# Behind the attention: x loaded early, norms' chains as bursts with a root step of third order, normed tiles turned and logits formed half a step later

## The chip, the core and the metric

The kernel runs on 1 core of one Trainium2 chip. It is one program with one launch. The metric is the device time of that core in microseconds (us); lower is better. A run of the kernel gives one time, and the median of several runs is what counts.

## What is computed

Two layers over 8 x 56 = 448 tokens of width 256 (S = 56), with a context of 1500 rows for each of the 8 batches. Cut to what matters here:

```python
x = x + attention0(layernorm(x), ctx)      # 16 heads of 128, softmax over 1500 keys, then @ Wo
x = x + moe0(layernorm(x))                 # 8 experts of 176 units, 2 chosen, plus 352 shared units
x = x + attention1(layernorm(x), ctx)      # linear attention, 16 heads of 16, 64 features, biases
x = x + moe1(layernorm(x))                 # 8 experts, 2 chosen, plus 704 shared units with a sigmoid gate

def moe(x):
    probs = softmax(x @ router)            # the two largest are kept; moe1 divides them by their sum
    h = silu(x @ w_gate) * (x @ w_up)      # all experts side by side: 1408 + shared columns
    return (h * weight_of_its_expert) @ w_down
```

layernorm subtracts the mean and multiplies by 1 / sqrt(variance + 1e-5).

## The kernel before

The program has three parts. The first forms sums over the context for the linear attention, and queries. The second is the softmax attention of layer 0, batch by batch, in a loop that all engines share. The third, from about 1034 us on, is what follows the attention: the output projection with Wo, three more norms, two mixtures of experts and the linear attention between them. All the edits lie in the third part and at the end of the second. Products there use a value split into a high and a low part and three matmuls (`mm3`, L104 to L106), so each weight and each activation has a high copy, made by ScalarE, and a low rest, made by VectorE or GpSimd.

**Tokens.** The 448 tokens are four tiles of 112 (`TP`), x is held as `[112, 4, 256]`, and the third part works on two halves (h = 0, 1) of two tiles each. A half's norm, router, linear attention and expert products follow each other; the halves are staggered, so that the small work of one half lies beside the expert products of the other.

**Output projection.** `wo.project(t, i)` forms tile t from quarter i of the heads, 12 matmuls each, t by t. `wo.add` (L1018) adds x to two finished tiles. The first norm (`ln1`) of half 0 is turned on TensorE between tiles 2 and 3. x is loaded by SyncE (L1783) behind the first layer's expert weights (L1290 to L1294: gate, up and down, 1.8 MB each, and 96 rows of down on their own) and behind a wait for the last output of the attention, since its tile takes the place of the attention's value weights.

**A norm** (class `Norm`): on VectorE `statistics` (L786, L789), `variance` (L803), a first value of the root (`guess`, L819, by the bits of the number; for the first half of the first norm ScalarE does it by Ln and Exp, L809 and L811), three Newton steps (`sharpen`: L828, L830, L833 each; one step after ScalarE's value), `apply` (L840, two tiles). Then `turn` on TensorE (L849), and from its PSUM bank `high` (L864) and `copy` (L869) on ScalarE and `low` (L876) on VectorE. Each small instruction waits for the one before it.

**A router** (class `Router`): `logits` (TensorE, L1140, from the norm's copy), `start` (VectorE, L1178 to L1183), `exponentials` (ScalarE, L1157 and L1159), `shares` (L1190 to L1194), `ranks` (L1203 to L1209), `weights` (L1216 to L1232), `turn` (TensorE, L1149), `high` (ScalarE, L1165), `low` (VectorE, L1171). ScalarE switches its table for Exp and again for Silu.

**Experts** (class `Experts`): the units are blocks of 128, 14 blocks in the first layer and 17 in the second. Step k is one block for one half; the steps go layer by layer, half by half: 28 and 34. For a step: `widen` (TensorE, 12 matmuls of gate and up), `silus` (ScalarE, L1411), `hidden` (VectorE, L1432), `spread` (TensorE, L1388, the token weights laid over the units), `weigh` (VectorE, L1444), `high` (ScalarE, L1423), `low` (VectorE, L1451), `narrow` (TensorE, 6 matmuls of down). `widen` of step k needs `hidden` of step k - 2. Weights of a block are split by `split_high` (ScalarE, L1340, L1343, L1346) and `split_low` (GpSimd, L1354, L1357, L1360).

**The order** is written out by hand: every engine runs a loop over positions n = 0 to 63 and does at each position the pieces that the functions `widen_at`, `spread_at`, `narrow_at` and `split_at` and the `if` lines give it. Step k is widened at position k, and as a rule spread there and narrowed three positions later. Position 28 (`FIRST1`) is where the second layer's steps begin, 45 (`SECOND1`) where those of its second half do. The second norm, the linear attention (`lin.query` L1539, `features`, `read`, `project`) and the third norm of half h sit at r = n - `BASE[h]`, with BASE = (15, 30). An engine runs its queue in order: whatever waits holds all that is behind it.

The last norm's first half is turned at position 28 ahead of everything else there, between the down projections of steps 26 and 27.

## Time and profile before

| | us |
|---|---|
| median of 3 runs (lowest to highest) | 1268.29 (1268.07 to 1269.38) |
| the profiled execution | 1267.16 |
| its span, first to last instruction | 1265.3 |
| TensorE busy | 1183.0 (93%) |
| VectorE busy | 880.1 (70%) |
| ScalarE busy | 740.6 (59%) |
| GpSimd busy | 536.7 (42%) |
| mean granted clock of TensorE | 0.982 of full speed |
| the part from 1034 us on | 231 |

The profile is one execution, recorded instruction by instruction. "Busy" is the time in which an engine has an instruction under way; a matmul's record reaches past the start of the next one, since they are pipelined. The granted clock is 1.0 at TensorE's higher level (2.4 GHz) and half of that at the lower (1.2 GHz). An engine that waits is shown with the instruction that released it. PEld is TensorE's weight load and runs beside the matmuls. SPq is SyncE's queue, which issues the transfers.

### The profile page before, as it was taken

Reading aid. Unit: us, or ns where it says so; the run is one execution under the profiler, and the core shown is the slowest. Engines: PE = TensorE matmul, PEld = TensorE weight load, DVE = VectorE, ACT = ScalarE, POOL = GpSimd, SP = SyncE. Lnnn points to the kernel's source line nnn. Section 1 sums busy time; section 2 is a strip of 40 time slices with the busy share of each in tenths; the row PEclk is TensorE's granted clock in tenths of the full one; section 3 lists DMA queues with packets and bytes.
Section 4 is the critical chain, followed back from the end, with each engine's and each line's share of the span. In section 5 each row is a group of like instructions: output and inputs, shape, how many; then the busy total and the mean of one; then the engine's idle time right before and its main releaser. Section 6 shows DMA issues by size and latency. Waiting matters only on the chain.

```text
span 1265.3 us, 28266 instructions
## 1 busy us (share of the span) xinstructions
PE 1183.0 (93%) x10014; PEld 1055.5 (83%) x10014; DVE 880.1 (70%) x1950; ACT 740.6 (59%) x1330; POOL 536.7 (42%) x561
## 2 busy tenths in 40 slices
PE   5999999999969999999999999999999996998988
PEld 4899999998848888888788788887888896887888
DVE  5766666666657888878878788788777643666564
ACT  3666666666545666576566665765666643544432
POOL 1533232323235363553643635535445764634400
PEclk9999999999989999999999999999999998999999
DMA  4211111100031111011010110111001024023000
GB/s 144 76 43 57 41 40 50 56 26 1 2 102 46 49 50 50 1 49 49 28 38 31 49 49 0 49 49 37 11 0 51 18 112 127 2 68 109 1 9 9
DMA packets 42689, 56.12 MB, mean 44 GB/s; under 512 B 3410, under 2 KB 41602, under 8 KB 42626
## 3 DMA queue, kind: packets, MB, share of 16 engines
q1 hardware_dynamic: 41810, 54.23, 13.6%
q10 hardware_dynamic: 816, 1.05, 0.3%
q8 instruction: 40, 0.66, 0.2%
q14 instruction: 23, 0.19, 0.0%
HBM read 54.81 MB, written 0.46 MB: 44 GB/s over the span
## 4 chain that ended last, share of the span: by engine, by line
PE 57%; DVE 7%; DMA 2%; issue 2%; ACT 2%; SPq 1%; POOL 1%; DVEq 0%; ACTq 0%
PE att_bank L104 16%; PE att_bank L106 15%; PE att_bank L105 15%; PE att_bank L1858 6%; PE att_bank L1816 3%; DMA att_raw_n<-in_ctx 1%; DVE att_cn L2113 1%; DVE att_pr L2167 1%; DMA tail_x<-in_x 1%; SPq L1294 1%; DVE tail_full L1432 1%; PE att_bank L1570 1%; DVE tail_hid L1451 0%; PE att_bank L943 0%; PE att_bank L1388 0%
## 5 line engine op out<-in xcount | busy, mean ns | idle before, releaser
L2339 POOL TENSOR_TENSOR att_sq<-att_work,att_sq 128x500 fp32r<-128x500 f32 x90 | 119.9, 1332 | 159.9 <-DVE att_sq L2133 159.9
L2343 POOL TENSOR_TENSOR attention_kk<-att_work,attention_kk 128x500 fp32r<-128x500 f32 x90 | 121.9, 1355 | 153.9 <-DVE attention_kk L2141 153.9
L104 PE MATMUL att_bank<-att_pT,att_cn 125*128 125x448 f32 x384 | 156.9, 409 | 5.5 <-DVE att_pT L2182 4.8
L1996 ACT ACTIVATE att_pr<-att_pr,att_nmx 112x1500 f32<-112x1500 f32 (+1 forms) x96 | 108.5, 1130 | 71.8 <-DVE att_nmx L2170 71.8
L106 PE MATMUL att_bank<-att_pT,att_cn 125*128 125x448 f32 x384 | 140.8, 367 | 0.0
L105 PE MATMUL att_bank<-att_pT,att_cn 125*128 125x448 f32 x384 | 140.4, 366 | 0.0
L2182 DVE TENSOR_TENSOR att_pT<-att_bank,att_pT 125x448 fp32r<-125x448 f32 x192 | 118.2, 616 | 14.6 <-ACT att_pT L2012 14.3
L2167 DVE TENSOR_SCALAR_CACHE_REDUCE att_pr<-att_bank 112x500 f32<-112x500 f32 x192 | 121.7, 675 | 6.3 <-PE att_bank L106 4.9
L1858 PEld LDWEIGHTS att_bank<-all_ident,att_pr 112*125 112x125 f32 x768 | 109.6, 189 | 14.2 <-ACT att_pr L1996 2.1
L538 DVE SCALAR_TENSOR_TENSOR attention_kk<-kvs_keys_ps,kvs_bk,attention_kk 64x500 fp32r<-64x500 f32 x96 | 70.9, 738 | 61.2 <-ACT attention_kk L422 59.3
L1858 PE MATMUL att_bank<-all_ident,att_pr 112*125 112x112 f32 x768 | 111.2, 271 | 1.7 <-ACT att_pr L1996 1.7
L293 PE MATMUL kvs_feat<-kvs_f,attention_kk 128*125 128x256 f32 x768 | 108.0, 283 | 4.5 <-ACT kvs_kp L475 4.3
L1985 ACT ACTIVATE att_work<-att_bank,att_eps 128x500 f32<-128x500 f32 x90 | 60.7, 675 | 86.7 <-PE att_bank L106 86.7
L2012 ACT ACTIVATE att_pT<-att_bank 125x448 fp32r<-125x448 f32 x192 | 102.2, 532 | 12.2 <-PE att_bank L1858 12.2
L681 POOL TENSOR_TENSOR attention_ct<-attention_raw_t,attention_ct 128x1000 fp32r<-128x1000 f32 x23 | 53.9, 2342 | 117.2 <-ACT attention_ct L414 117.2
L293 PEld LDWEIGHTS kvs_feat<-kvs_f,attention_kk 128*125 128x125 f32 x768 | 98.0, 187 | 6.2 <-ACT kvs_kp L475 4.0
L475 ACT ACTIVATE kvs_kp<-kvs_feat,kvs_zero 125x512 f32<-125x512 f32 x96 | 66.1, 689 | 59.7 <-PE kvs_feat L293 58.5
L2136 DVE TENSOR_TENSOR att_work<-att_bank,att_work 128x500 f32<-128x500 f32 x90 | 60.9, 676 | 56.4 <-ACT att_work L1992 55.7
L422 ACT ACTIVATE attention_kk<-kvs_keys_ps,kvs_bk 64x500 fp32r<-64x500 f32 x96 | 64.7, 674 | 52.6 <-PE kvs_keys_ps L106 51.2
L104 PE MATMUL att_bank<-attention_kk,attention_q 128*112 128x500 f32 x192 | 77.6, 404 | 17.1 <-DVE att_pr L2167 11.9
L1990 ACT ACTIVATE att_work<-att_bank,att_eps 128x500 f32<-128x500 f32 x90 | 61.1, 679 | 46.2 <-PE att_bank L1816 46.2
L104 PEld LDWEIGHTS att_bank<-att_pT,att_cn 125*128 125x128 f32 x384 | 73.2, 191 | 15.7 <-DVE att_pT L2182 9.9
(279 smaller groups left out, 3418.9 us busy)
## 6 DMA issues: line engine op xcount, KB each, us to landing
attention_raw_t<-in_ctxT SPq DMA_DIRECT2D x45, 500.0 KB, 3.9
att_raw_n<-in_ctx SPq DMA_DIRECT2D x16, 750.0 KB
kvs_raw_q<-in_wq SPq DMA_DIRECT2D x8, 256.0 KB, 3.9
tail_wo_raw<-in_wo SPq DMA_DIRECT2D x4, 512.0 KB, 4.4
tail_down_w<-in_down SPq DMA_DIRECT2D x8, 256.0 KB, 4.2
tail_gate_w<-in_gate SPq DMA_DIRECT2D x7, 256.0 KB, 2.8
tail_up_w<-in_up SPq DMA_DIRECT2D x7, 256.0 KB, 3.2
tail_gate_w<-in_gate SPq DMA_DIRECT2D x1, 1760.0 KB, 7.0
```

The lines of the kernel that those rows point to most:

```text
L104: nc.tensor.matmul(out, w_lo, x_hi, start=start, stop=False, skip_group_check=True)
L105: nc.tensor.matmul(out, w_hi, x_lo, start=False, stop=False, skip_group_check=True)
L106: return nc.tensor.matmul(out, w_hi, x_hi, start=False, stop=stop, skip_group_check=True)
L293: last = nc.tensor.matmul(feat[0:KP, half, z], ks[:, c, 2 * half + g, y], f2[:, w, :], start=(w == 1), stop=(w == 0), skip_group_check=True)
L538: nc.vector.scalar_tensor_tensor(ks[64:128, c, 2 * m + h, :], keys_ps[y, 0:CH], bk[y, m:m + 1], ks[0:64, c, 2 * m + h, :].bitcast(F32), AL ...
L1858: last = nc.tensor.transpose(ring[0:KP, t % 3, j * TP:(j + 1) * TP], pr[:, j, t * KP:(t + 1) * KP], ident[0:TP, 0:TP])
L1996: nc.scalar.activation(pr[:, j, keys], pr[:, j, keys], ACT.Exp, scale=-1.0, bias=nmx[:, j:j + 1], accum_out=z[:, 4 * u + j, c:c + 1]).then ...
L2012: nc.scalar.activation(pT[0][:, t % 3, :], ring[0:KP, t % 3, 0:QU], ACT.Copy).then_inc(pT_hi, 1)
L2167: nc.vector.tensor_scalar(pr[:, j, c * CH:(c + 1) * CH], ring[0:TP, c, 0:CH], -1.0, 3.0e38, ALU.mult, ALU.min, accum_out=mn[:, j, c:c + 1] ...
L2182: nc.vector.tensor_tensor(pT[1][:, t % 3, :], ring[0:KP, t % 3, 0:QU], pT[0][:, t % 3, :].bitcast(F32), ALU.subtract).then_inc(ring_free, 1)
L2339: nc.gpsimd.tensor_tensor(sq[1][:, i % 2, :], work[:, i % 2, :], sq[0][:, i % 2, :].bitcast(F32), ALU.subtract).then_inc(sq_lo, 1)
L2343: nc.gpsimd.tensor_tensor(kk[:, c, 2 + gi, :], work[:, i % 2, :], kk[:, c, gi, :].bitcast(F32), ALU.subtract).then_inc(k_lo, 1)
```

## The change

- x is loaded by SyncE as soon as two quarters of Wo are split (`wo_lo[1]`, `wo_lo[2]`), ahead of the expert weights. Its tile moves to the place of those quarters' raw weights.
- The first layer's expert weights are loaded as a head (5 blocks of gate, up and down) and a rest. A split of one of the first five blocks waits for all three head loads, a later one for all four of the rest.
- ScalarE does three weight splits, not two, ahead of the first root value, and the fifth one ahead of the first router's exponentials.
- `refine` takes the place of three `sharpen`: a step of third order in four instructions and one of second order in three, 7 in place of 9. For ln1's half 1, ln2 and ln3, statistics, root and normed tiles stand in one position and no longer in two (in ln1's half 1 the statistics stay two positions ahead).
- `ln2.turn` moves up within its position, ahead of the down projection, and `lin.query` to the end of the same position (half a position earlier). The rest of the linear attention comes one position earlier.
- `ln3`: its chain at r = 10, turned at r = 12 ahead of the down projection, logits at the end of r = 12. The router's start and exponentials are first in position r = 13, shares and ranks last in it; the weights come first in r = 14, the turn in the middle of r = 14. Half 0's turn, formerly at the head of position 28, is now handled as half 1's is.
- Down projections of steps 24 to 27 lie at positions 27, 28, 29 (behind the router's turn) and 29. The spreads of the second half's first steps are no longer held back to positions 48 to 50.
- Weight splits move a little: those of positions 14 to 16 to 12 to 14; 25, 28 and 31 are free, 26, 29, 30 and 32 to 38 are used.

```diff
-        return 4 if h == 0 and self.scalar_first else 11
+        return 4 if h == 0 and self.scalar_first else 9
...
+    def refine(self, dve, h):
+        nc, y, n = self.nc, self.half(h), self.first(h) + 2
+        rstd, tmp, var = self.rstd[:, y], self.tmp[:, y], self.var[:, y]
...
+        nc.vector.tensor_tensor(tmp, rstd, rstd, ALU.mult).then_inc(self.newton, 1)
+        nc.vector.tensor_tensor(tmp, tmp, var, ALU.mult).then_inc(self.newton, 1)
+        nc.vector.scalar_tensor_tensor(tmp, tmp, -10.0 / 3.0, tmp, ALU.add, ALU.mult).then_inc(self.newton, 1)
+        nc.vector.scalar_tensor_tensor(rstd, tmp, 5.0, rstd, ALU.add, ALU.mult).then_inc(self.newton, 1)
+        nc.vector.tensor_tensor(tmp, rstd, rstd, ALU.mult).then_inc(self.newton, 1)
+        nc.vector.scalar_tensor_tensor(tmp, tmp, -0.5 * 0.375 ** 3, var, ALU.mult, ALU.mult).then_inc(self.newton, 1)
+        nc.vector.scalar_tensor_tensor(rstd, tmp, 0.5625, rstd, ALU.add, ALU.mult).then_inc(self.newton, 1)
...
 def spread_at(k):
-    late = {0: 1, FIRST1: 29, SECOND1: 48, SECOND1 + 1: 48, SECOND1 + 2: 49, SECOND1 + 3: 49, SECOND1 + 4: 50}
-    return late.get(k, widen_at(k))
+    return {0: 1, FIRST1: FIRST1 + 1}.get(k, widen_at(k))
 def narrow_at(k):
-    return {FIRST1 // 2 - 1: k + 2, FIRST1 - 2: FIRST1, FIRST1 - 1: FIRST1, len(STEPS) - 1: k + 2}.get(
-        k, k + 3 if spread_at(k) == k else spread_at(k) + 2)
+    return {0: k + 3, FIRST1 // 2 - 1: k + 2, FIRST1 - 1: k + 2, len(STEPS) - 1: k + 2}.get(k, k + 3)
...
+        if m == 0 and n < HEAD:
+            act.wait_ge(self.head_loaded, 48)
+        elif m == 0:
+            act.wait_ge(self.rest_loaded, 64)
...
+        x = over_raw("x", [TP, TT, D])
...
+            sp.wait_ge(wo.wo_lo[1], 1)
+            sp.wait_ge(wo.wo_lo[2], 1)
+            sp.dma_start(x[:], a["x"].rearrange("(t p) d -> p t d", p=TP)).then_inc(x_loaded, 16)
             sp.wait_ge(pv_done, 2 * B * KT)
             sp.wait_ge(wo.wo_lo[3], 1)
-            moe.load_first(sp, a["gate0"], a["up0"], a["down0"])
-            sp.wait_ge(out_full, 2 * B)
-            sp.dma_start(x[:], a["x"].rearrange("(t p) d -> p t d", p=TP)).then_inc(x_loaded, 16)
+            moe.load_head(sp, a["gate0"], a["up0"], a["down0"])
+            moe.load_rest(sp, a["gate0"], a["up0"], a["down0"])
...
@@ TensorE's loop, in its new order
                 if n == FIRST1 + 1:
                     router.turn(pe, 2)
+                    moe.narrow(pe, FIRST1 - 2)
...
+                    if r == 3:
+                        ln2.turn(pe, h)
...
+                    if r == 12:
+                        ln3.turn(pe, h)
+                    if r == 14 and h == 1:
                         router.turn(pe, 3)
                 for k in steps_at(narrow_at, n):
...
                     if r == 3:
+                        lin.query(pe, h)
+                    if r == 12:
+                        router.logits(pe, 2 + h, ln3)
...
@@ ScalarE
+                for h in range(H):
+                    if n - BASE[h] == 13:
+                        router.exponentials(act, 2 + h)
+                if n == FIRST1 + 1:
+                    router.high(act, 2)
                 for k in steps_at(widen_at, n):
                     moe.silus(act, k)
...
@@ VectorE
+                for h in range(H):
+                    r = n - BASE[h]
+                    if r == 13:
+                        router.start(dve, 2 + h)
+                    if r == 14:
+                        router.weights(dve, 2 + h)
+                if n == FIRST1 + 1:
+                    router.low(dve, 2)
                 for k in steps_at(widen_at, n):
                     moe.hidden(dve, k)
...
                         ln2.statistics(dve, h, moe.added, h + 1)
                         ln2.guess(dve, h)
-                        ln2.sharpen(dve, h, 0)
+                        ln2.refine(dve, h)
                         ln2.apply(dve, h)
...
                     if r == 12:
+                        ln3.low(dve, h)
+                    if r == 13:
+                        router.shares(dve, 2 + h)
+                        router.ranks(dve, 2 + h)
```

## Rows read from the trace of the kernel before

**Rows 1.** Waits after 1034 us: total us, times, longest

```profile
PE att_bank L849 <- DVE tail_scratch L840: 16.8, 6, 8.7
```

**Rows 2.** Stages: us; PE, PEld, DVE, ACT, POOL busy; PEclk; DMA

```profile
1051.20:1069.10 17.90, 9.23 (x61) 9.23 (x62) 7.21 (x19) 6.83 (x19) 8.85 (x14) 0.71 0.24 60
...
1150.00:1168.00 18.00, 12.35 (x89) 11.31 (x88) 11.56 (x46) 9.91 (x24) 4.60 (x7) 0.91 0.42 131
...
1209.00:1229.00 20.00, 16.15 (x126) 15.23 (x126) 10.76 (x44) 7.91 (x16) 0.00 (x0) 0.91 0.00 1
```

**Rows 3.** Timeline of TensorE: start us, us, operation, [idle before <-releaser]

```profile
1045.27 0.28 PE L106 MATMUL att_bank<-tail_wo,tail_o_high 128*112 128x256 f32 x1
...
1050.89 0.28 PE L106 MATMUL att_bank<-tail_wo,tail_o_high 128*112 128x256 f32 x1
...
1059.87 1.01 PE L849 MATMUL att_bank<-all_ident,tail_scratch 112*128 112x112 f32 x4 [8.70 <-DVE tail_scratch L840]
...
1060.89 0.41 PE L105 MATMUL att_bank<-tail_wo,tail_o_high 128*112 128x256 f32 x1
...
1064.73 0.41 PE L105 MATMUL att_bank<-tail_wo,tail_o_high 128*112 128x256 f32 x1
```

**Rows 4.** Timeline of VectorE and ScalarE: the first norm's chain

```profile
1054.41 0.69 DVE L1018 TENSOR_TENSOR tail_x<-tail_x,att_bank 112x512 f32<-112x512 f32 x1 [10.50 <-DMA tail_x<-in_x]
...
1056.52 0.29 ACT L809 ACTIVATE tail_ln_rstd<-tail_ln_var,tail_zero 112x2 f32<-112x2 f32 x1 [2.40 <-DVE tail_ln_var L803]
...
1058.30 1.51 DVE L840 TENSOR_SCALAR tail_scratch<-tail_x,tail_ln_mv,tail_ln_rstd 112x256 f32<-112x256 f32 x2
```

**Rows 5.** GpSimd, SyncE, ScalarE; transfers (KB each, us to landing)

```profile
1028.81 4.75 POOL L980 TENSOR_TENSOR tail_wo<-tail_wo_raw,tail_wo 128x1024 fp32r<-128x1024 f32 x2
...
1033.65 0.37 SPq L1290 DMA_DIRECT2D tail_gate_w<-in_gate  x1
...
1041.83 0.95 ACT L986 ACTIVATE tail_o_high<-all_qT 128x896 fp32r<-128x896 f32 x1 [7.94 <-DVE all_qT L1001]
...
1052.78 0.42 ACT L1346 ACTIVATE tail_high_w<-tail_down_w 128x256 fp32r<-128x256 f32 x1 [5.88 <-DMA tail_down_w<-in_down]
...
tail_gate_w<-in_gate SPq DMA_DIRECT2D x1, 1760.0 KB, 7.0
...
tail_x<-in_x SPq DMA_DIRECT2D x1, 448.0 KB, 11.3
```

**Rows 6.** Timeline of TensorE at ln2's turns

```profile
1116.01 0.28 PE L1388 MATMUL att_bank<-tail_combT,tail_member 128*128 128x224 f32 x1
...
1119.15 0.60 PE L849 MATMUL att_bank<-all_ident,tail_scratch 112*128 112x112 f32 x4 [2.17 <-DVE tail_scratch L840]
...
1176.52 0.60 PE L849 MATMUL att_bank<-all_ident,tail_scratch 112*128 112x112 f32 x4 [3.12 <-DVE tail_scratch L840]
```

**Rows 7.** Timeline of VectorE in the norms' chains

```profile
1174.07 0.57 DVE L830 SCALAR_TENSOR_TENSOR tail_ln_tmp<-tail_ln_tmp,tail_ln_var 112x2 f32<-112x2 f32 x1
...
1207.19 0.74 DVE L786 BATCH_NORM_STATS2 tail_ln_stats<-tail_x 112x6 f32<-112x256 f32 x2
...
1208.59 0.16 DVE L828 TENSOR_TENSOR tail_ln_tmp<-tail_ln_rstd 112x2 f32<-112x2 f32 x1
```

**Rows 8.** Timeline around the second layer's routers

```profile
1156.34 0.18 DVE L1178 COPY tail_logit<-att_bank 112x18 f32<-112x18 f32 x1 [0.33 <-PE att_bank L1140]
...
1157.48 1.28 ACT L1411 ACT_TABLE_LOAD   x1
...
1158.78 0.45 ACT L1411 ACTIVATE tail_silu<-att_bank,tail_zero 128x224 f32<-128x224 f32 x1
...
1162.18 0.36 PE L1149 MATMUL att_bank<-all_ident,tail_comb 112*9 112x112 f32 x2 [3.11 <-DVE tail_comb L1232]
...
1223.67 0.28 DVE L1216 TENSOR_REDUCE tail_places<-tail_rank 112x16 f32<-112x128 f32 x1
...
1225.12 0.36 PE L1149 MATMUL att_bank<-all_ident,tail_comb 112*9 112x112 f32 x2 [1.30 <-DVE tail_comb L1232]
```

More of the change, by code:

```diff
@@ L1919, in _ @@
             for n in range(POSITIONS):
-                if n == FIRST1:
-                    moe.narrow(pe, FIRST1 - 3)
-                    moe.narrow(pe, FIRST1 - 2)
-                    ln3.turn(pe, 0)
-                    moe.narrow(pe, FIRST1 - 1)
-                    router.logits(pe, 2, ln3)
                 for k in steps_at(widen_at, n):
@@ L1965, in _ @@
                     if r == 3:
-                        ln2.turn(pe, h)
-                    if r == 13 and h == 1:
-                        ln3.turn(pe, 1)
-                        router.logits(pe, 3, ln3)
+                        lin.query(pe, h)
+                    if r == 12:
+                        router.logits(pe, 2 + h, ln3)
         @block.scalar
@@ L2047, in _ @@
             moe.split_high(act, 1)
+            moe.split_high(act, 2)
             ln1.guess_on_scalar(act, 0)
[L2049 removed]
+            moe.split_high(act, 3)
             ln1.high(act, 0)
             ln1.copy(act, 0)
[L2052 removed]
+            moe.split_high(act, 4)
             router.exponentials(act, 0)
[L2054 removed]
             for n in range(POSITIONS):
[L2056 to L2060 removed]
+                for h in range(H):
[3 more added lines that the diff above has]
+                    router.high(act, 2)
                 for k in steps_at(widen_at, n):
                     moe.silus(act, k)
[L2063 to L2064 removed]
                 if n == 1:
@@ L2072, in _ @@
                     router.high(act, 1)
-                if n == BASE[1] + 17:
-                    router.high(act, 3)
                 for i in split_at(n):
@@ L2085, in _ @@
                         ln2.copy(act, h)
+                        lin.query_on_scalar(act, h)
                     if r == 4:
-                        lin.query_on_scalar(act, h)
+                        lin.feature_on_scalar(act, h, 0)
                     if r == 5:
-                        lin.feature_on_scalar(act, h, 0)
-                    if r == 6:
                         lin.feature_on_scalar(act, h, 2)
-                    if r == 9:
+                    if r == 8:
                         lin.copy(act, h)
-                    if r == 13 and h == 1:
+                    if r == 12:
+                        ln3.copy(act, h)
                         ln3.high(act, h)
-                        ln3.copy(act, h)
                     if r == 14 and h == 1:
-                        router.exponentials(act, 3)
+                        router.high(act, 3)
         @block.vector
@@ L2243, in _ @@
             for n in range(POSITIONS):
-                if n == FIRST1:
-                    moe.low(dve, FIRST1 - 1)
-                    ln3.low(dve, 0)
-                    router.start(dve, 2)
-                    router.shares(dve, 2)
-                    router.ranks(dve, 2)
+                for h in range(H):
[6 more added lines that the diff above has]
+                    router.low(dve, 2)
                 for k in steps_at(widen_at, n):
                     moe.hidden(dve, k)
-                if n == FIRST1:
-                    router.weights(dve, 2)
-                if n == FIRST1 + 1:
-                    router.low(dve, 2)
                 if n == 1:
@@ L2260, in _ @@
                 for k in range(len(STEPS)):
[L2261 removed]
+                    if spread_at(k) + 1 == n:
                         moe.low(dve, k)
@@ L2264, in _ @@
                     router.low(dve, 1)
-                if n == BASE[1] + 17:
-                    router.low(dve, 3)
                 if n == 0:
```

118 lines of the change are left out of this document (45 added, 73 removed).

## The prediction

> **What bounds it now.** I read the page's engine shares first, then the waits after the attention, then the stages, and last the timeline of each long wait. TensorE bounds the kernel, and up to 1034 us the diff touches nothing but one load. After 1034 us TensorE still has nearly all the work, in a fixed order, so what can be won is the time in which it stands still or runs at the lower of its two clocks. [rows 1] shows where: its longest waits are for the normed tile (L840, 16.8 us in 6 waits), and one transfer holds VectorE for 10.5 us [rows 4]; next come TensorE's waits for the routing weights (L1232) [rows 8]. [rows 2] shows three stages of 18 to 20 us in which it is busy for 9.2, 12.4 and 16.2 us, with a granted clock of 0.71, 0.91 and 0.91. The rest of the tail is dense. I therefore treat matmul work as unchanged and sum the idle and slow time, counting each wait from the start that a gapless stream would have had (about 0.15 us before the printed wait begins, since a matmul's end lies behind the next one's start).
>
> **Part A: x loaded early, first weights cut in two.** TensorE's last matmul of the third tile starts at 1050.89 and the turn at 1059.87; at the stream's step of 0.118 us that is 8.9 us lost. Then matmuls last 0.41 us instead of 0.28 and come every 0.213 us: 22 of them lose 22 x 0.095 = 2.1 us, and the turn takes 0.69 where 0.39 would do, 0.3 us. Together 11.3 us [rows 3].
> The cause is one wait: the addition L1018 starts when x lands at 1054.41 although the last matmul it needs had ended at 1045.55 [rows 3, 4]. Now x follows the second and third split of wo, so SyncE can issue it at about 1028.81 + 4.75/2 = 1031.2 [rows 5]; it took 11.3 us behind 5 MB of weights [rows 5], and even that would land it at 1042.5. VectorE's chain from the addition to the last normed tile is 1059.81 - 1054.41 = 5.4 us [rows 4], so the tile is ready at 1045.6 + 5.4 = 1051.0, when TensorE comes for it. I book 0.2 us of remaining wait, 11.1 us gained.
> What the early landing may meet: the seed of the root (L809) now stands behind three weight splits on ScalarE instead of two, and each needs all three head loads. ScalarE is busy with o_high until 1042.78 [rows 5]. The head is 1.97 MB; the gate load of 1.80 MB landed 7.0 us after its issue at 1033.65 [rows 5], so the head should be in at about 1041 to 1042. Nine splits at a step of 0.31 us end at 1045.6; the seed is asked for 2.1 us after the addition [rows 4], at 1047.7. So this edit costs nothing up to a landing at 1044.9, and one for one after. Bounds for A: 10.0 (a slower head or slower small VectorE instructions) to 11.4. The rest of the first weights is wanted only behind the first silu, at 1060; all the loads were in by 1052.8 [rows 5].
> The wait after the first router (2.0 us, for L1171) is set by ScalarE's two splits ahead of its high part; these stay, so it stays, and so does the slow stretch behind it.
>
> **Part B: the first norm's second half.** The whole root and the normed tile now come in one burst a position earlier. 7 instructions at a step of 0.20 us [rows 7] hold VectorE for 1.4 us where 9 in two pieces stood; that is 0.4 us less work, under TensorE's cover. The wait of 0.61 us before that turn (1 of the 6) goes: 0.8 us with its tail. TensorE has about 3 us until it needs what the burst delays.
>
> **Part C: ln2, first half.** Before: the spread at 1116.01 and six more matmuls end the stream at 1116.83, the turn comes at 1119.15, 2.3 us lost [rows 6]; the 12 matmuls behind it run at the slow step of [rows 3] and lose 1.2: 3.5 us. Now the turn stands ahead of those six, so it is asked for at 1116.12. The burst takes 3.5 us from the first statistics to the last tile: 1.4 us to the first root step [rows 7], 1.4 for seven steps, 0.7 for two tiles. It starts at 1114.2 and ends at 1117.75, so the turn waits 1.65. Then a new wait: the query needs ScalarE's copy of the turned tile, and ahead of that copy ScalarE's queue has the high part of a step whose weighing stands behind the burst. From the tile: hidden, weigh 0.8, high 0.3, copy 0.5, 2.1 us in all with the steps between them; TensorE has 1.15 us of work. New wait 0.95. Sum 2.6 plus a slow stretch of 0 to 1.4 us, the two sizes met in the trace (I take 1.0, since two waits come close together): 3.6. Gain 0.0, bounds -0.4 and 1.0.
>
> **Part D: ln3 and router, first half.** Before: lost 0.6, 1.0 and 0.6 at the end of the first expert layer, 3.4 before the router's turn at 1162.18, 1.0 for its two parts: 6.5 us, and 1.6 us of slow clock by the stage's figure, (1 - 0.91) x 18 [rows 2, 8]. Now, counted from the end of the gate and up products of position 25: silu, hidden and low take 1.3 us, the burst 3.5: complete at 4.85. TensorE gets there at 4.1 (two wide products of 12 x 0.111 us, two narrow ones of 6 x 0.118), so 0.75 is lost. The turn ends at 5.5, ScalarE's copy at 6.05 (TensorE's narrow product is done at 5.95, 0.15 lost) and its high part at 6.5, VectorE's low part at 7.1 (logits done at 6.9, 0.3 lost). Then the chain that decides. Its old form ran start, exponentials, shares, ranks without a break, and the turn came 1162.18 - 1156.34 = 5.8 us after the start [rows 8]. In its new form VectorE has the next step's hidden product between start and shares, and that product waits for ScalarE: exponentials, then the silu table (1.28 us, L1411 [rows 8]), then the silu. So: start at 7.1, exponentials done 8.2, table 9.5, silu 10.0, product and low part 10.6, shares and ranks 1.8 to 12.5, weights 1.8 to 14.3. TensorE, with two wide products and one narrow, is there at 10.55: a wait of 3.8, longer than the old one. The two parts of the turned weights are mostly covered by the narrow product put there (0.25). Sum 5.25, slow stretch as before; gain 1.25. GpSimd's split at position 26 now meets the burst's end; beside such a split VectorE's L830 took 0.57 us at 1174.07, where L828 took 0.16 [rows 7], and I take off 0.6. D: 0.7, bounds -0.5 and 1.6.
>
> **Part E: ln2, second half.** As C, but before lost 3.3 us and 1.2 of slow clock, 4.5 in all [rows 6]. The splits at positions 32 and 33 now stand there: GpSimd's runs all through the burst (1.0 us by the excess of L830 and its neighbours), ScalarE's of 0.9 us stands before the copy. The turn waits 2.25, the query 1.5, slow 1.3: 5.05. Loss 0.5, bounds -1.0 and 0.6.
>
> **Part F: ln3 and router, second half.** Before: turn 1.6, logits 1.3, router 1.5, and 1.7 slow: 6.1 us; the chain of 10 us from start to turn had four wide products over it [rows 2, 8]. Now it gets two, and takes, from the normed tile: start 2.7, exponentials 3.9, table 5.2, silu and product 6.1, weigh and low part 6.8, shares and ranks 8.5, weights 1.4 (1225.12 - 1223.67 [rows 8]) to 9.9. TensorE, after logits (2.5), two wide products, two spreads and a narrow one, is there at 6.15. Waits 0.9 + 0.6 + 3.75, slow 2.2: 7.5. Loss 1.4, bounds -2.7 and 0. The spreads that were held back to positions 48 to 50 move, not grow; no wait stands there before.
>
> **Sum.** 11.1 + 0.8 + 0.0 + 0.7 - 0.5 - 1.4 = 10.7 us. The profiled execution took 1267.16 (span 1265.3 and 1.9 around it), so the new one is 1256.5; the median of the runs is 1.13 above the profiled one, which gives 1257.6. The bounds add to 6.0 and 15.4 us (B 0.6 to 0.8): 1252.9 to 1262.3.
>
> **Two rules weighed.** A table load shows 1.28 us here and the silu starts 1.30 us after it [rows 8]. The Trainium skill, ScalarE: Activation LUTs, What ACT_TABLE_LOAD costs, puts about 1.38 us of drain on top of each. This speaks against the change, since D and F put the second load of each router on the chain; by it the gain would be 10.7 - 2 x 1.38 = 7.9, and the trace does not bear it out. VectorE's small root steps rise from 0.16 to 0.57 us while GpSimd subtracts [rows 7]. The Trainium skill, SBUF — State Buffer, Who interferes with whom, lets such pairs block each other; by it E's burst would pay at each of GpSimd's three instructions, which is what I took.
>
> **Rivals.**
> (1) The routing chains are no longer than the old one (5.8 us): D and F each wait 1.4 less, and with shorter waits the slow stretches of C and E go, 2.0 more. Gain 15.5, 1252.8. For it: slow stretches are missing after the single waits of 1.4 us; against: the queue order. Chance 0.12.
> (2) The bursts and GpSimd hurt more: each router 1.2 us longer and both slow stretches full, gain 6.9, 1261.4. For it: before, three weight instructions took 0.5 to 0.65 us beside a split. Chance 0.13.
> (3) The head lands at 1050, and 5 us of A are lost: 1262.6. For it: ScalarE waited to 1052.78 for the last down rows [rows 5]. Chance 0.05. The same mechanism is the slow side: from a landing at 1044.9 + 10.7 = 1055.6 on, the seed behind three splits eats the whole gain; at 1058 it is 2.4 us slower than before, 1270.7. Chance 0.01.
> (4) The silu starts 1.4 us behind its table load instead of right behind it [rows 8], once on each router's chain: gain 7.9, 1260.4. Chance 0.02. (This is the rule on the table load above.)
> Forecast 0.67. The range 1252.8 to 1261.8 takes in (1), (2) and (4). Faster by over 0.2% (2.5 us, about what can be told from no change here) 0.98, within 0.01, slower 0.01.
>
> **What would show it.** Right: L1018 starts near 1045.6 and no wait before the first L849; L1149 waits of near 4 us, both of them, led by L1232; new waits of 1 to 1.5 us before L1539; VectorE's L1432 between L1183 and L1190 with the table load ahead of it. Wrong: an L809 that waits for splits, L1149 waits under 2.5 us, or slow stretches missing.

## The result and the profile of the changed kernel

| | us, median | lowest to highest | executions |
|---|---|---|---|
| before | 1268.18 | 1267.2 to 1269.59 | 6 |
| changed | 1258.86 | 1256.55 to 1262.91 | 6 |

The ratio is 0.9928, with a 95% interval of 0.991 to 0.9946: 9.3 us faster. The forecast was 1257.6, with a range of 1252.8 to 1261.8. The profiled execution of the changed kernel took 1257.69 us, its span 1255.2.

TensorE's waits after the attention, in us in all, times, longest; of the changed kernel. It answers [rows 1]:

```profile
PE att_bank L868 <- DVE tail_scratch L859: 8.8, 5, 2.8
PE att_bank L1161 <- DVE tail_comb L1244: 3.9, 2, 2.2
PE att_bank L1161 <- DVE tail_comb L1234: 2.4, 1, 2.4
PE att_bank L1403 <- DVE tail_combT L1183: 2.0, 1, 2.0
```

The waits for a normed tile fell from 16.8 us to 8.8: the 8.7 us wait of [rows 3] is now 1.62. Lines have moved by 12 to 19: L849 is now L868, L840 is L859, L1018 is L1037, L1149 is L1161, L1232 is L1244, L1539 is L1554.

A better comparison than sums of waits is the time between the same two matmuls of TensorE, since its work between them is the same but for one piece (below the table). I took the first matmul of the output projection (1032.71 before, 1033.57 changed) and the first gate product of expert steps 0, 17, 25, 33 and 57. Two of these for the changed kernel (timeline of TensorE):

```profile
1060.63 0.26 PE L104 MATMUL att_bank<-tail_xn,tail_gate_low 128*128 128x224 f32 x1
...
1236.32 0.27 PE L104 MATMUL att_bank<-tail_xn,tail_gate_low 128*128 128x224 f32 x1
```

| stretch, us | before | changed | changed, second profile | gain | forecast |
|---|---|---|---|---|---|
| projection to step 0 | 36.38 | 27.06 | 27.00 | 9.3, 9.4 | A 11.1 |
| step 0 to 17 | 43.42 | 42.69 | 42.72 | 0.7, 0.7 | B 0.8 |
| 17 to 25 | 30.33 | 30.32 | 30.32 | 0.0, 0.0 | C 0.0 |
| 25 to 33 | 28.25 | 26.54 | 25.71 | 1.7, 2.5 | D 0.7 |
| 33 to 57 | 75.36 | 76.14 | 77.93 | -0.8, -2.6 | E and F -1.9 |
| all | 213.74 | 202.75 | 203.68 | 11.0, 10.1 | 10.7 |

Steps 17 to 25 and 25 to 33 do not hold the same work in the two kernels. The output projection of the linear attention's first half, 8 matmuls, lies behind step 25's first gate product before, and ahead of it in the changed kernel (kernel before, then changed; the next down projection starts at 1145.71 and at 1132.73):

```profile
1144.17 1.89 PE L1594 MATMUL att_bank<-tail_lin_wo,tail_attT 128*112 128x256 f32 x8
```

```profile
1131.20 1.89 PE L1609 MATMUL att_bank<-tail_lin_wo,tail_attT 128*112 128x256 f32 x8
```

It holds TensorE for 1.5 us in both. On equal work the gain of steps 17 to 25 is therefore 1.5 us and not 0.0, and that of steps 25 to 33 is 0.2 (first profile) and 1.0 (second).

The second profile is a run of the same kernel made later (below). The output projection with Wo starts anywhere from 1032.7 to 1034.5 in the profiles of this study, without an order between kernels; that is scatter of the attention, which the change does not touch.

The first norm's chain in the changed kernel, on VectorE and then on GpSimd beside it (start us, us). It answers [rows 4]:

```profile
1046.51 0.69 DVE L1037 TENSOR_TENSOR tail_x<-tail_x,att_bank 112x512 f32<-112x512 f32 x1 [1.74 <-PE att_bank L106]
...
1048.24 1.04 DVE L803 TENSOR_SCALAR tail_ln_var<-tail_ln_mv 112x2 f32<-112x2 f32 x1
1050.05 0.62 DVE L828 TENSOR_TENSOR tail_ln_tmp<-tail_ln_rstd 112x2 f32<-112x2 f32 x1 [0.76 <-ACT tail_ln_rstd L811]
1050.70 0.66 DVE L830 SCALAR_TENSOR_TENSOR tail_ln_tmp<-tail_ln_tmp,tail_ln_var 112x2 f32<-112x2 f32 x1
1051.40 0.66 DVE L833 SCALAR_TENSOR_TENSOR tail_ln_rstd<-tail_ln_tmp,tail_ln_rstd 112x2 f32<-112x2 f32 x1
1052.09 1.51 DVE L859 TENSOR_SCALAR tail_scratch<-tail_x,tail_ln_mv,tail_ln_rstd 112x256 f32<-112x256 f32 x2
```

```profile
1048.78 0.48 POOL L2390 MEMSET tail_combT<- 128x448 f32 x1
...
1049.90 0.76 POOL L1372 TENSOR_TENSOR tail_up_low<-tail_up_w,tail_high_w 128x256 fp32r<-128x256 f32 x1
1050.59 0.75 POOL L1375 TENSOR_TENSOR tail_down_low<-tail_down_w,tail_high_w 128x256 fp32r<-128x256 f32 x1
1051.29 0.75 POOL L1369 TENSOR_TENSOR tail_gate_low<-tail_gate_w,tail_high_w 128x256 fp32r<-128x256 f32 x1
```

x is there: the addition waits for TensorE and no longer for a transfer. But the chain takes 1053.60 - 1046.51 = 7.1 us where it took 5.4. Read the ends (start plus length): L828 ends at 1050.67, L830 at 1051.36, L833 at 1052.06, and the three GpSimd subtractions end at 1050.66, 1051.34 and 1052.04. L803 ends at 1049.28, the memset at 1049.26. Each of these small VectorE instructions lasts until the GpSimd instruction beside it is over.

The routing waits, and the clock ahead of them. First the changed kernel, by windows (from:to, length, busy of PE, PEld, DVE, ACT, POOL, granted clock, DMA share, GB/s) and timeline, then the second profile of the same kernel:

```profile
1201.60:1207.00 5.40, 5.40 (x35) 5.17 (x34) 2.75 (x12) 3.49 (x7) 0.00 (x0) 0.68 0.02 5
1209.20:1214.00 4.80, 4.80 (x43) 4.79 (x44) 2.33 (x7) 1.30 (x4) 0.00 (x0) 1.00 0.00 0
...
1209.16 0.36 PE L1161 MATMUL att_bank<-all_ident,tail_comb 112*9 112x112 f32 x2 [2.16 <-DVE tail_comb L1244]
```

```profile
1201.60:1205.30 3.70, 3.70 (x34) 3.52 (x33) 1.14 (x6) 3.38 (x7) 0.00 (x0) 1.00 0.02 7
1209.10:1213.90 4.80, 4.80 (x29) 4.75 (x30) 1.65 (x5) 1.07 (x3) 0.00 (x0) 0.65 0.00 0
...
1209.10 0.54 PE L1161 MATMUL att_bank<-all_ident,tail_comb 112*9 112x112 f32 x2 [3.76 <-DVE tail_comb L1244]
```

The turn comes 7.6 and 7.5 us behind the window's start. In the first profile TensorE does the work ahead of it at a mean granted clock of 0.68 (part of it at the lower level), needs 5.4 us for it and waits 2.16; in the second it has the full 2.4 GHz, needs 3.7 and waits 3.76. Here the slow stretch that ends in a wait costs nothing, and the one behind the wait (0.65, second profile) does: steps 33 to 57 take 77.93 us there and 76.14 in the first profile.

### The profile page after: what moved, and what is told of

Same layout as the page of the kernel before. It is cut to its first block, busy times and chain, and to the rows that moved or that the text cites. A ratio compares the mean times of both kernels' runs of the same rounds, so it can differ in the third digit from the quotient of the medians.

```text
span 1255.2 us, 28260 instructions
## 1 busy us (share of the span) xinstructions
PE 1180.6 (94%) x10014; PEld 1052.7 (84%) x10014; DVE 881.0 (70%) x1940; ACT 739.6 (59%) x1330; POOL 536.2 (43%) x561
## 4 chain that ended last, share of the span: by engine, by line
PE 60%; DVE 6%; ACT 2%; issue 1%; DMA 1%; DVEq 0%; SPq 0%; ACTq 0%
PE att_bank L104 17%; PE att_bank L106 15%; PE att_bank L105 15%; PE att_bank L1877 6%; PE att_bank L1835 3%; DMA att_raw_n<-in_ctx 1%; DVE att_cn L2123 1%; DVE att_pr L2177 1%; PE att_bank L1585 1%; PE att_bank L962 1%; DVE tail_hid L1466 0%; DVE tail_full L1447 0%; PE att_bank L1554 0%; ACT att_work L2007 0%; PE att_bank L1403 0%
## 5 line engine op out<-in xcount | busy, mean ns | idle before, releaser
L104 PEld LDWEIGHTS att_bank<-att_pT,att_cn 125*128 125x128 f32 x384 | 73.1, 190 | 15.8 <-DVE att_pT L2192 10.1
```

What stands on the lines that cost most here:

```text
L104: nc.tensor.matmul(out, w_lo, x_hi, start=start, stop=False, skip_group_check=True)
```

## The experiments

Each kernel was timed beside the kernel before on one chip. Medians of before in the three groups were 1268.70 (the first four), 1269.15 (the next four) and 1267.82 (the last two). There are 4 to 6 executions of each kernel, 12 of no head and of x late.

| kernel | us, median | lowest to highest | ratio to before, 95% |
|---|---|---|---|
| x early alone | 1258.15 | 1257.36 to 1259.91 | 0.9916 (0.9903 to 0.9929) |
| root in three steps | 1263.45 | 1261.25 to 1266.19 | 0.9961 (0.9946 to 0.9975) |
| GpSimd aside | 1254.18 | 1252.62 to 1258.63 | 0.9889 (0.9873 to 0.9905) |
| shares early | 1256.08 | 1252.42 to 1259.34 | 0.9888 (0.9871 to 0.9905) |
| both edits | 1246.71 | 1245.89 to 1250.19 | 0.9834 (0.9817 to 0.9851) |
| no head | 1265.45 | 1263.29 to 1266.65 | 0.9973 (0.9964 to 0.9982) |
| x late | 1268.07 | 1265.48 to 1270.23 | 0.9994 (0.9983 to 1.0004) |
| both and two more | 1245.30 | 1244.60 to 1246.83 | 0.9814 (0.9799 to 0.9829) |
| no moves | 1255.45 | 1252.76 to 1255.96 | 0.9894 (0.9879 to 0.9909) |
| changed, again | 1258.56 | 1257.52 to 1261.17 | 0.9929 (0.9915 to 0.9942) |

**Which part carries the gain.** The first part alone, on the kernel before:

```diff
+            sp.wait_ge(wo.wo_lo[1], 1)
+            sp.wait_ge(wo.wo_lo[2], 1)
+            sp.dma_start(x[:], ...).then_inc(x_loaded, 16)
...
-            moe.load_first(sp, a["gate0"], a["up0"], a["down0"])
-            sp.wait_ge(out_full, 2 * B)
-            sp.dma_start(x[:], ...).then_inc(x_loaded, 16)
+            moe.load_head(sp, a["gate0"], a["up0"], a["down0"])
+            moe.load_rest(sp, a["gate0"], a["up0"], a["down0"])
```

> The kernel before with the first part of the change alone: x in its new place and loaded behind the third split of the output weights, the expert weights as a head of 5 blocks and a rest, ScalarE's roots before the fourth split. The chains, their order and the turns stay as before. My theory (the early x is worth less than the 11.1 us I booked, because the first norm's chain on VectorE now runs beside GpSimd's subtractions): from the first matmul of the output projection to the first expert matmul 27.0 us, as in the changed kernel (27.06), against 36.38 before; the chain from the addition to the end of the applied norm takes about 7 us; and since the other parts of the change together moved the end by only 0.1 us, the time is 1258 to 1259.5, the same as the changed kernel's 1258.9. Rival (the early x is worth its 11.1 us or more, and the bursts and later turns give some of it back): 1256 to 1257.5.

Measured 1258.15, and 27.06 us from the projection to step 0, as expected: everything else in the change adds nothing to the time that can be told from noise (the intervals of the two ratios overlap). Its turn waits 1.62 us too. The other side, the changed kernel with x behind the head and the rest:

> The changed kernel with x loaded behind the head and the rest, after the last batch's output as in the kernel before; place of x, head and all else stay. Theory (nearly the whole gain of the change hangs on when x lands): the addition starts near 1054 as before instead of 1046.5, GpSimd's first splits are then nearly done and the chain takes 5.4 us instead of 7.1, so the first turn is 6 us later, and the slow stretch behind it comes back: 1258.9 + 6.2 to 7.7 = 1265 to 1266.6. Rival (x lands at about 1048, since the transfers ahead of it are nearly through by the time it is issued): 1259.5 to 1261.5.

```profile
1054.99 0.69 DVE L1037 TENSOR_TENSOR tail_x<-tail_x,att_bank 112x512 f32<-112x512 f32 x1 [10.61 <-DMA tail_x<-in_x]
```

Measured 1268.07, no difference from the kernel before that can be told. x lands no earlier than in [rows 4]. I had the place right and the sum 1.5 us low: the turn waits 8.63 us, and slow clock behind it costs 2.7 us (6.20 us from 1060.3 on at a granted clock of 0.56), where I had allowed 1.5. And the head cut taken back, with x early:

> The changed kernel with the first expert's weights loaded whole again, in the four transfers of the kernel before and with its three separate waits; x stays early and everything else stays. Theory (the head of 5 blocks matters because ScalarE's roots stand behind three weight splits): the first down block lands about 1052.7 as before, the splits of blocks 0 to 2 end about 1054.5, the roots start there instead of at 1049.3, and the first turn comes about 5.5 us later: 1258.9 + 5.5 = 1264.4. Rival (the whole load lands early enough, since nothing but x is ahead of it): the roots wait for the variance still, 1258 to 1260.

```profile
1042.70 0.40 ACT L1352 ACTIVATE tail_high_w<-tail_gate_w 128x256 fp32r<-128x256 f32 x1
1046.44 0.42 ACT L1355 ACTIVATE tail_high_w<-tail_up_w 128x256 fp32r<-128x256 f32 x1 [3.33 <-DMA tail_up_w<-in_up]
1051.90 0.42 ACT L1358 ACTIVATE tail_high_w<-tail_down_w 128x256 fp32r<-128x256 f32 x1 [5.04 <-DMA tail_down_w<-in_down]
...
1054.06 0.28 ACT L809 ACTIVATE tail_ln_rstd<-tail_ln_var,tail_zero 112x2 f32<-112x2 f32 x1
```

Measured 1265.45. The seed L809 stands behind the three splits and starts at 1054.06 where it started at 1049.32. So the early x needs the head: without it 6.6 us of the 9.3 are lost.

**What makes the chain 7.1 us.** The changed kernel, with GpSimd waiting at three places:

```diff
             moe.split_low(pool, 0)
+            pool.wait_ge(ln1.xn_done, 2)
             moe.split_low(pool, 1)
...
+                if i == 21:
+                    pool.wait_ge(ln3.xn_done, 2)
+                if i == 24:
+                    pool.wait_ge(ln2.xn_done, 4)
                 moe.split_low(pool, i)
```

> The changed kernel with GpSimd stepping aside for three bursts: it waits for the first half of the first norm to be applied before its second weight split, and in the same way for the third norm's first half before split 21 and for the second norm's second half before split 24. Nothing else moves. Theory (a small VectorE instruction takes 0.62 to 0.66 or 1.04 us instead of 0.16 only while a GpSimd subtraction runs): the first chain takes 4.2 us instead of 7.1, the small instructions are all at 0.16 to 0.17 us, and TensorE's waits of 1.63, 2.16 and 2.82 us before the turns become about 0, 0.7 and 1.4; time 1258.9 - 4.4 = 1254.5. Rival 1 (the clock takes it back: the slow stretch of 1.5 us that the kernel before had behind the first router's scales and the changed one has not returns, or others grow): waits as said, but 1256 to 1257.5. Rival 2 (the slow instructions have another cause, ScalarE's copies or the addresses): no wait shorter, the time 1258.9 or above it.

```profile
1048.10 0.17 DVE L803 TENSOR_SCALAR tail_ln_var<-tail_ln_mv 112x2 f32<-112x2 f32 x1
1049.03 0.16 DVE L828 TENSOR_TENSOR tail_ln_tmp<-tail_ln_rstd 112x2 f32<-112x2 f32 x1 [0.76 <-ACT tail_ln_rstd L811]
1049.22 0.16 DVE L830 SCALAR_TENSOR_TENSOR tail_ln_tmp<-tail_ln_tmp,tail_ln_var 112x2 f32<-112x2 f32 x1
1049.42 0.16 DVE L833 SCALAR_TENSOR_TENSOR tail_ln_rstd<-tail_ln_tmp,tail_ln_rstd 112x2 f32<-112x2 f32 x1
1049.62 0.73 DVE L859 TENSOR_SCALAR tail_scratch<-tail_x,tail_ln_mv,tail_ln_rstd 112x256 f32<-112x256 f32 x2
```

Measured 1254.18; expected 1254.5. The small instructions are all at 0.16 or 0.17, the two applied tiles take 0.73 us together instead of 1.51, the first turn has no wait, and the other two waits are 0.74 and 0.84 (from 2.16 and 2.82). The chain takes 4.0 us, less even than the 5.4 of the kernel before. From the projection to step 0 it is now 25.19 us: 11.2 less than before, about what I had booked for part A. The rest of its profile is not as clean as the time suggests. Steps 0 to 17 and 17 to 25 take 44.16 and 32.00 us, 1.5 and 1.7 more than in the changed kernel, though the waits there are the same (2.36 before the second router's turn, 1.47 before ln2's): slow clock came in behind both. Steps 25 to 33 take 26.31 us, hardly less than 26.54, since all the slow clock around the third routing now stands behind its turn (3.4 us, 10.00 us from 1149 on at 0.66), where half of it stood ahead of the wait. The profile's gain lies in steps 33 to 57 (72.34 us from 76.14) and in the first stretch.

The Trainium skill, SBUF — State Buffer, Who interferes with whom, has VectorE instructions with two SBUF inputs contend with a GpSimd instruction that reads SBUF; of the two-port modes, which tensor_scalar can enter, it says that "Whoever issues first gets the shared pair for the whole instruction". The ends read above agree: L828, L830 and L833 end with GpSimd's subtractions, and the tensor_scalar L803 with the memset.

**What makes the routing waits.** The changed kernel, with one block moved up VectorE's queue:

```diff
                     if r == 13:
                         router.start(dve, 2 + h)
+                        router.shares(dve, 2 + h)
+                        router.ranks(dve, 2 + h)
```

> The changed kernel with the shares and ranks of the third and fourth routing directly behind their start on VectorE, ahead of the hidden product that waits for SiLU and so for the second table load. Theory (the routing waits of 1.76 and 2.16 us are made by this place in VectorE's queue, not by the table loads themselves): the shares start 0.6 us after the start's last instruction instead of 3.4, the whole chain takes about 4.3 us instead of 7.05, both waits go, and the time is 1258.9 - 3.9 = 1255.0, or about 1253.5 if the slow clock behind the third routing goes with its wait. Rival (VectorE held for the exponentials and the ranks makes the hidden products late, and TensorE waits for those): the two waits go, others of 1 us or more appear within 4 us, and the time is 1257.5 to 1259.5.

Measured 1256.08, between the theory's 1255.0 and the rival's 1257.5. The third routing's wait is gone, the fourth's is still 1.96 us: its weights stand behind a hidden product that has to wait for SiLU and its table. So half of the theory held. The profiled execution, 1259.34, was the slowest of the five; slow clock around the third routing costs 3.4 us in it (21.40 us from 1146.6 on at 0.84), about as much as in the changed kernel. Hence the next kernel has both edits, and the weights moved up too:

> The two edits together, on top of the changed kernel: GpSimd steps aside for the three bursts, and on VectorE the whole third and fourth routing (shares, ranks and now the weights too) stands directly behind its start, ahead of the hidden product that waits for SiLU. Theory (the contention and the place in VectorE's queue are separate costs): against the run with GpSimd aside (1254.2) the routing waits of 2.99 and 2.31 us shrink to about 0.3 and 0.6, which gives 1254.2 - 4.4 = 1249.8. Rival 1 (the shorter waits only move work under a slower clock, as in the profile with the early shares, whose slow stretches held 3.6 us at one place): 1252 to 1254. Rival 2 (VectorE held 1.3 us longer by the weights makes the hidden products late): a new wait on a hidden product of over 0.5 us within 4 us behind each routing, 1251.5 or above.

Its waits, and the clock around the third routing, which turns at 1144.49:

```profile
PE att_bank L868 <- DVE tail_scratch L859: 4.4, 4, 1.5
...
PE att_bank L1161 <- DVE tail_comb L1244: 0.4, 1, 0.4
...
1138.30:1144.00 5.70, 5.43 (x47) 5.09 (x45) 4.92 (x19) 5.08 (x9) 2.10 (x3) 1.00 0.31 96
1144.50:1149.50 5.00, 4.86 (x41) 4.64 (x42) 2.62 (x8) 2.82 (x10) 2.12 (x3) 1.00 0.68 218
```

Measured 1246.71, 3 us better than the theory, and both rivals are out. Apart, the two edits gave 4.7 and 2.8 us; together, with the weights moved too, 12.2. The fourth routing's wait of 1.96 us, which the weights' place had kept, is 2 of the 4.7 us more. That anything is left to explain is not shown: by the ratios of the table, of which each is good to about 0.0018 (2.3 us), the edits gave 4.9 and 5.1 us apart and 11.9 together, and the wait covers the difference. What the profiles do show is that the slow clock went. In the changed kernel it was 0.76 and 0.53 around the third routing:

```profile
1141.60:1148.80 7.20, 7.03 (x47) 6.65 (x45) 3.80 (x15) 5.05 (x9) 0.00 (x0) 0.76 0.07 15
1150.60:1154.20 3.60, 3.60 (x19) 3.60 (x20) 1.45 (x4) 1.60 (x5) 2.10 (x3) 0.53 0.19 64
```

In the changed kernel and in the two kernels with one edit, slow clock around this routing cost 3.4 us each; here it costs nothing (1.00 in both windows). Steps 25 to 33 take 21.18 us, against 26.54 in the changed kernel and 28.25 before, where they hold 1.5 us more work.

Two more moves of this kind:

```diff
-                if n == 9:
+                if n == 8:
                     router.shares(dve, 1)
...
-    after = {0: (5, 6), 1: (7,), ...
+    after = {1: (5, 6), 2: (7,), ...
```

(ranks and weights likewise one step up.)

> The kernel with both edits, and two more of the same kind: the shares, ranks and weights of the second routing one step earlier on VectorE (steps 8, 9 and 10 instead of 9, 10 and 11), and ScalarE's splits of blocks 5, 6 and 7 one step later, behind the copy of the first routing's scales. Theory: the wait of 2.36 us before the second routing's turn goes, and the wait of 2.0 us before the first spreading of the scales shrinks to about 1.0; against the kernel with both edits -3.4 us, about 1246.4. Rival (the clock takes back what the waits give): -1 us or less against it, with more slow stretches. Second rival (split 5 or 6 is then late): a wait for the low part of the weights of over 0.5 us before step 5.

Measured 1245.30, the fastest kernel here, but only 1.4 us under the one before it, with intervals that overlap, and 191.2 against 191.5 us from the projection to step 57. The wait of 2.36 us went, the one before the first spreading shrank only from 2.01 to 1.79 us instead of to 1.0, and two others came: 1.1 us before the second turn, and this one, for a hidden product that stands behind the ranks, which in turn run beside GpSimd's splits (0.56 to 0.82 us each instead of 0.29):

```profile
1091.64 0.34 PE L104 MATMUL att_bank<-tail_xn,tail_gate_low 128*128 128x224 f32 x1 [1.84 <-DVE tail_full L1447]
...
1088.45 0.82 DVE L1215 TENSOR_TENSOR tail_rank<-tail_prob 112x128 f32<-112x128 f32 x1
```

My theory for this one is wrong: the wait did not go, it changed its name. In this profile slow clock costs 1.7 us at the third routing again (12.00 us from 1138 on at 0.86), with no wait before its turn, so the absence of that wait does not rule such a stretch out.

**What the root step and the moves are worth.** The changed kernel with `sharpen` three times in place of `refine`:

> The changed kernel with the root of the norms in three steps of second order again (nine small VectorE instructions behind the guess in place of seven), still in one burst, at the same places. If the waits before the turns of normed tiles end with the burst, each of the four that TensorE waits for grows by two instructions of about 0.2 us: the waits of 1.47, 2.16, 2.82 and 0.77 us become 1.9, 2.6, 3.2 and 1.2, and the time is 1258.9 + 1.6 = 1260.5. Rival (the bursts are covered, or TensorE's clock takes the difference up): under 1259.3.

Measured 1263.45, 4.6 us above the changed kernel's 1258.86, three times what I expected. The waits grew as computed (1.86, 2.56, 3.20 and 1.17 us). The rest is slow clock. Around the turn of the second norm's first half, this kernel, and then the changed one (second profile):

```profile
1109.00:1113.00 4.00, 3.68 (x16) 3.21 (x17) 2.50 (x6) 0.82 (x2) 1.29 (x1) 0.63 0.35 103
```

```profile
1109.10:1113.00 3.90, 3.47 (x24) 3.29 (x25) 2.45 (x6) 1.18 (x3) 1.28 (x1) 1.00 0.39 113
```

Steps 17 to 25 take 32.07 us instead of 30.32, behind a wait 0.4 us longer. But that the longer wait brings the slow stretch is not shown: with GpSimd aside and with shares early the wait is 1.47 us, as in the changed kernel, and the stretch is there all the same (32.00 us in both).

Last, the first part with the third-order bursts (`refine` where the first `sharpen` stood), and nothing else moved:

> The kernel before with the early x and the head (as in the run of the first part alone, 1258.15) and with the third-order root in one burst with the applied norm, at the place where the first step stood; the turns, the query, the logits, the readout and the routing stay where the kernel before has them. It shows what the moves of parts C to F are worth by themselves. Theory (the bursts are the gain, and the moves of the readout and of the turns spend it): against 1258.15 the waits before the turns shrink, in order of time, from 1.31 to 0, from 2.18 to about 0.8, from 0.79 to 0, from 3.32 to about 2.1 and from 1.43 to 0, together 6 us, so 1252 to 1254, below the changed kernel. Rival (the moves are what makes the bursts pay; the waits of the routing, 3.1 and 1.8 us, grow by what the turns give): 1256.5 to 1259.

```profile
1143.36 0.35 PE L104 MATMUL att_bank<-tail_high_w,tail_hid 128*112 128x256 f32 x1 [2.04 <-DVE tail_hid L1473]
```

Measured 1255.45, between the theory and its rival and 3 us below the changed kernel. The waits before the turns went as computed or further (0, 0.81, 0, 0 and 0 us), but the third norm's first burst made the low part of a hidden tile late, 2.04 us of new wait, and the third routing's wait stayed at 2.97. The moves of the turns, the readout and the routing thus cost 3.1 us against this kernel (1258.56 to 1255.45, timed together, with intervals that do not overlap). The 2.7 us that the bursts with the root step bring (1258.15 to 1255.45) were timed in different groups, and their intervals overlap. The turns' waits shrank by more than that: in the two profiles slow clock costs about 7 us from step 0 to 57 in x early alone and about 12 here, so much of what the waits gave was paid back.

**The spread.** The changed kernel again:

> The changed kernel once more, word for word, beside the run without the moves, for its spread: its first six executions reached from 1256.6 to 1262.9 while the kernel before stayed within 2.4 us. Theory (its spread is TensorE's clock: the same waits each time, but slow stretches behind them that come or stay away): the slower executions show a granted clock of 0.980 to 0.983 and the faster ones 0.985 or more, each 0.001 worth about 1 us; the waits of the profiled execution agree with the first profile within 0.1 us unless a slow stretch lies before them. Rival (something else scatters, a transfer or GpSimd): times that do not follow the clock, or a wait on TensorE that the first profile has not.

Of the 11 executions of the changed kernel, the four above 1259.5 us had granted clocks of 0.980, 0.980, 0.981 and 0.983, the seven below it 0.984 to 0.987. The waits of the two profiles agree within 0.05 us up to 1141 us and, where the clock ahead of them differed, add up to about the same (above). I take the spread for the clock's; this is a correlation, and no run sets the clock. "0.001 worth 1 us" holds roughly: 1256.55 came at 0.984 and 1258.9 at 0.987.

## Why the prediction was right, point by point

The time and the direction were right, and the sum of the tail too (10.7 against 11.0 and 10.1). The two largest misses go in opposite directions, so it is partly luck that the sum came out this close: A gave 1.8 us less than booked, C 1.5 more.

- **What bounds it, and the cause of the long wait: right.** With x late the whole gain is gone.
- **Part A: mechanism right, 11.1 booked, 9.3 measured.** The step that failed is "VectorE's chain from the addition to the last normed tile is 1059.81 - 1054.41 = 5.4 us". I took its length from a place where GpSimd held up only part of it (L833 and the normed tiles, while L828 and L830 took 0.16); moved 8 us up, it meets the splits of blocks 0 to 3, and L803, L828 and L830 are held too. That is 1.62 us of wait where I booked 0.2. I had named "slower small VectorE instructions" as the lower bound of 10.0 and had seen them in [rows 7], but did not lay GpSimd's timeline beside the chain's new place. 9.3 lies below even that bound. With GpSimd aside the term is 11.2.
- **The head: right.** The splits follow o_high without a wait, and the rival that the head lands late is out. The run without the cut shows that the rival's mechanism is real and its size near the 5 us given for it (6.6 us).
- **Part B: right,** 0.8 against 0.7. But the slow stretch behind the first router, which I left standing, is missing in both profiles of the changed kernel (1.7 us, 8.00 us from 1073 on at 0.79 in the kernel before); the wait before the second router's turn, which I left at 1.4, is 2.36, and a new one of 0.60 stands behind the burst. These cancel, which is luck too.
- **Part C: wrong, 0.0 booked, 1.5 measured on equal work,** above its bound of 1.0. The stretch's 0.0 hides this, since the linear attention's projection moved into it. The step that failed is the slow stretch, "I take 1.0, since two waits come close together", with the query's wait: the turn waits 1.47 (1.65 booked), the query 0.42 (0.95), and no slow clock follows in either profile.
- **Parts D, E and F: -1.2 together, measured -0.6 and -1.6 on equal work.** The turn's wait in D is 2.16 us where I had 0.75: three root instructions at 0.62 to 0.65 us beside the split of position 26 (I took off 0.6, it is 1.4). The routing chain of D is 7.1 and 7.4 us from start to turn in the two profiles, that of F 7.3 in both, forecast 7.2. (The "10 us from start to turn" of F's old chain are counted from the end of its logits; from L1178 at 1218.21 to the turn it was 6.9.) What failed is "Sum 5.25, slow stretch as before", and "slow 2.2" in F: I added slow clock to a wait that absorbs it. In the first profile slow clock costs 1.7 us ahead of D's wait of 1.76 (7.20 us at 0.76) and 1.7 ahead of F's 2.16 (5.40 at 0.68): 3.5 and 3.9 together, near the 3.8 and 3.75 of the forecast. In the second profile F's wait is 3.76. So my sign of a wrong forecast, "L1149 waits under 2.5 us", was met three times of four, although the chains were as I had them and the total came out: a wait is what is left when the other side has arrived, and I should have named the time from start to turn.
- **E's query wait** is 0.3 to 0.6 us, not 1.5; the lower clock stands in its place there too.
- **The table load: the trace was right against the page.** Nothing of the drain of about 1.38 us that the Trainium skill, ScalarE: Activation LUTs, What ACT_TABLE_LOAD costs, puts on top of a load shows in the changed kernel (timeline of ScalarE), and rival 4 is out:

```profile
1203.05 1.28 ACT L1426 ACT_TABLE_LOAD   x1
1204.35 0.45 ACT L1426 ACTIVATE tail_silu<-att_bank,tail_zero 128x224 f32<-128x224 f32 x1
```

- **Rival 1 did not come in:** the chains are 7 us long.
- **Not settled:** the slow stretch behind the first router stands in seven of the twelve profiles of this study and not in the other five; which it is depends on something that these runs do not tell apart.

## What to carry to other kernels

A chain of tiny VectorE instructions that is moved in time takes its length from its new neighbours: look at what GpSimd does at the new place before you price it, and let GpSimd wait for the chain rather than the other way round if its splits have slack (one wait instruction at each of three places gave 4.7 us). Put short work of one chain directly behind the instruction that starts it, ahead of anything in the same queue that waits for a third engine, and check what it delays: at the second routing the wait only moved. Price a wait by the two arrivals, not by itself: slow clock ahead of a wait was free here, slow clock behind it was paid. And when you compare two kernels between the same two instructions, count what lies between them first: a piece of work that crossed the mark hid 1.5 us of gain.

## What the runs showed of the hardware

- A VectorE instruction on 112x2 elements in SBUF takes 0.16 us alone and 0.62 to 0.66 beside a GpSimd subtraction, and it ends within 0.02 us of the end of that subtraction. L803, a tensor_scalar, sat through the end of one and a 0.48 us memset, 1.04 us in all. L830 and L833, which read two SBUF tiles, took 0.16 us each beside such a memset (1055.21 and 1055.41, no head). GpSimd's instruction keeps its 0.75 us. Products with one input in PSUM kept their time: a hidden product L1447 took 0.37 to 0.39 us throughout the changed kernel.
- A slow stretch of TensorE's clock came and went behind the same 1.47 us wait: steps 17 to 25 took 30.32 us without it (both profiles of the changed kernel) and 32.00 with it (GpSimd aside, shares early). An effect of under 2 us can so be lost or doubled in one profile.
- The spread of one kernel's times (6.4 us over 11 executions) goes with its granted clock (0.980 to 0.987); the fastest kernel, with the shortest waits in all, has the highest clock (0.989 to 0.990) and the smallest spread of the changed ones (2.2 us). A high clock is not needed for a small spread: the kernel before spread over 2.4 us in its first six executions.
